# Four-block vision megakernel on one Trainium2 core: the channel norm moved into the projection's block and cut by bank, one ScalarE table set for logarithm and exponential, and image 1's delta sum taken per chunk inside its scan

## The reference

```python
x = x + L0(gn(x), ...)   # region normalization against bicubic maps
x = x + L1(gn(x), ...)   # 9-neighbour similarity graph, weighted sum, two 1x1 products
x = x + L2(gn(x), ...)   # Mamba block over the 4096 pixels as tokens
x = x + L3(gn(x), ...)   # deformable 3x3 convolution
```

```python
mu = mean(xf, -1); var = mean(square(xf - mu), -1)          # over the 32 channels of a token
xn = (xf - mu) * rsqrt(var + 1e-05) * ln_w + ln_b
xin, z = split(xn @ W_in.T)                                 # 64 + 64
u = silu(causal_conv4(xin) + conv_b)
dt, Bm, Cm = split(u @ W_xproj.T)                           # 2, 16, 16
delta = softplus(dt @ W_dt.T + b_dt)
# per token: h = exp(delta * A) * h + delta * u * B;  y = sum(h * C)
y = (ys + u * D) * silu(z);  out = y @ W_out.T
```

## Time and profile before

| | |
|---|---|
| runs | 1011.0 us median of 3 (1010.9 to 1011.95) |
| profiled execution | 1014.24 us, its span 1012.0 us |
| busy share of the span | PE 77%, VectorE 83%, POOL 57%, ScalarE 38% |
| mean granted TensorE clock | 0.832 of full speed |
| stages, us from the span's start | L0 to 50, L1 to 137, norm of L2 to 162, projection 0 to 205, scan 0 to 342, start of L3 to 368, projection 1 to 424, scan 1 to 671, L3 of image 1 to 1012 |

### The profile page before, as it was taken

The page is one execution under the profiler, slowest core; times in us unless marked ns, Lnnn a source line. Parts: engine busy times, 40 slices in busy tenths (PEclk is TensorE's granted clock), DMA queues, the critical chain, the costliest instruction groups (busy, mean ns, idle before and its releaser), DMA issues.

```text
span 1012.0 us, 8286 instructions
## 1 busy us (share of the span) xinstructions
PE 782.5 (77%) x2365; PEld 377.3 (37%) x2365; DVE 837.1 (83%) x1161; ACT 387.0 (38%) x544; POOL 580.1 (57%) x528
## 2 busy tenths in 40 slices
PE   2345875677787688676788787869379999999997
PEld 1132322222222124534454444423264444444443
DVE  3889842789999858879998899985989998979884
ACT  1120046854454136311212121101049586776650
POOL 0000000076765037877777777777777777777774
PEclk9666987979999889567777677776559999999998
DMA  5000017000000361111111111128353745444422
GB/s 122 0 0 1 0 31 155 17 0 1 1 1 0 64 133 49 37 52 53 51 50 52 52 49 53 51 64 195 110 139 90 195 136 143 122 123 130 120 65 53
DMA packets 32339, 69.82 MB, mean 69 GB/s; under 512 B 12368, under 2 KB 12624, under 8 KB 31184
## 3 DMA queue, kind: packets, MB, share of 16 engines
q1 hardware_dynamic: 16080, 35.27, 13.2%
q0 software_dynamic: 15360, 31.49, 12.1%
q10 hardware_dynamic: 864, 2.64, 1.2%
HBM read 54.94 MB, written 5.77 MB: 60 GB/s over the span
## 4 chain that ended last, share of the span: by engine, by line
PE 42%; DVE 26%; POOL 7%; issue 6%; ACT 2%; DMA 1%; DVEq 0%; ACTq 0%; POOLq 0%
PE PS L1481 19%; POOL got L780 7%; DVE scratch L1174 6%; PE PS L815 5%; DVE scratch L1100 4%; DVE scratch L1181 3%; PE PS L1057 2%; PE PS L1042 2%; PE PS L1498 2%; DVE prodg L791 2%; PE PS L855 2%; DVE PS L1097 2%; PE PS L1274 2%; DVE prodg L795 1%; PE PS L914 1%
## 5 line engine op out<-in xcount | busy, mean ns | idle before, releaser
L780 POOL DMA_INDIRECT got<-corner_table,idx_slot x405 | 402.8, 995 | 123.4 <-issue 123.4
L1042 PE MATMUL PS<-parts,selb 96*128 96x512 bf16 (+1 forms) x256 | 88.4, 446 | 85.0 <-DVE scratch L1100 45.3
L1057 PE MATMUL PS<-scratch,wt 128*128 128x512 f32 x256 | 146.1, 701 | 0.5 <-DVE scratch L1181 0.5
L1481 PE MATMUL PS<-scratch,UZ 128*128 128x512 f32 (+1 forms) x288 | 133.6, 613 | 2.9 <-DVE scratch L1466 2.9
L780 POOL DMA_INDIRECT got<-corner_table,idx_all x75 | 84.9, 1132 | 60.6 <-DVE prime L1348 38.0
L821 ACT ACTIVATE G<-PS 128x32 f32 (+1 forms) x32 | 6.3, 197 | 250.7 <-PE PS L815 250.6
L815 PE MATMUL PS<-ln_g,w 128*128 128x32 f32 x576 | 101.9, 344 | 0.0
L815 PEld LDWEIGHTS PS<-ln_g,w 128*128 128x128 f32 x576 | 99.3, 268 | 0.0
L1564 POOL MEMSET w<- 128x1152 f32 x1 | 1.1, 1058 | 159.7 <-POOLq L599 159.7
L1042 PEld LDWEIGHTS PS<-parts,selb 96*128 96x128 bf16 x256 | 22.9, 116 | 158.2 <-DVE scratch L1100 59.1
L1458 ACT ACTIVATE scratch<-UZ,knot 128x512 f32<-128x512 f32 (+1 forms) x128 | 81.6, 708 | 0.4
(11 more groups left out here) (350 smaller groups left out, 1354.8 us busy)
## 6 DMA issues: line engine op xcount, KB each, us to landing
UZ<-dense_rows SPq DMA_DIRECT2D x24, 512.0 KB, 4.1
got<-corner_table,idx_slot POOLq DMA_INDIRECT x405, 2.5
UZ<-dense_rows SPq DMA_DIRECT2D x96, 64.0 KB, 2.2
XN<-ln_g SPq DMA_DIRECT2D x6, 256.0 KB, 5.8
got<-corner_table,idx_all POOLq DMA_INDIRECT x75, 2.5
corner_table<-scratch SPq DMA_DIRECT2D x1, 1056.0 KB, 10.4
corner_table<-XN SPq DMA_DIRECT2D x1, 1056.0 KB, 10.4
X<-in_x SPq DMA_DIRECT2D x4, 256.0 KB
```

The source lines that it names most:

```text
L780: pool.indirect_dma_start(got[:, slot, tap, :, :].rearrange("p k c -> p (k c)"), None, tables[b], bass.IndirectOffsetOnAxis(ap=index[:, ta ...
L1042: last = nc.tensor.matmul(PS[:, first + n, :], selb[:, which, j, :], parts[:, bass.ds(i * CHUNK + n * BANK, BANK)], start=True, stop=True)
L1057: last = nc.tensor.matmul(PS[:, 4 + n, :], wt[:, W_SUM:W_SUM + P], dBC[:, j % 2, n * BANK:(n + 1) * BANK], start=False, stop=(j == PAIRS - 1))
L1481: last = nc.tensor.matmul(PS[:, n % 4, :], steps[rows, j, :, :].rearrange("p b c -> p (b c)"), ramps[k][rows, j, :], start=(j == 0), stop= ...
```

## The change

Three edits, and a small one at the program's start. The norm's block is gone: its five instruction lists become `norm_sync`, `norm_tensor`, `norm_scalar`, `norm_vector`, which stand first in the lists of the fourth block. Within them g is made in four passes, the banks are interleaved, and ScalarE takes logarithm and exponential of one bank before it goes on; its temporaries are in `scratch`. ScalarE is told which table set to load at the start, in the norm and in the projection (`preload_act_table_set`). Image 1's delta sum moves from the end of its projection to the start of each turn of its scan, and its logarithm's buffer from `scratch` (which the scan uses) to XN's second image.

```diff
@@ first block, ScalarE
+                    nc.scalar.preload_act_table_set("sqrt_and_others")
                     act.dma_start(vec[:, :], vecs).then_inc(vec_in, 16)
                     act.dma_start(mat[:, 0:M_PAIR, :], mats[:, 0:M_PAIR, :]).then_inc(mat_in, 16)
                     act.dma_start(patch[32:64, :, :], anchors).then_inc(vec_in, 16)
@@ the norm: the block and its buffers go, four functions come
+        sq = scratch[:, 0:HALF]
+        selw = scratch[0:96, HALF:2 * HALF]
...
+        def norm_sync(sp):
+            sp.dma_start(selw, sel).then_inc(ln["sel_in"], 16)
+            sp.wait_ge(ln["zeroed"], 1)
+            for k in range(2):
+                sp.wait_ge(ln["xn_ready"], 2 * k + 2)
+                load_part(sp, k, range(4 - 2 * k))
+            sp.wait_ge(ln["sel_in"], 16)
+
+        def norm_tensor(pe):
...
+            def center(n):
+                pe.wait_ge(ln["g_ready"], n + 1)
+                nc.tensor.matmul(PS[:, n, :], M(M_CENTER), g[:, n * BANK:(n + 1) * BANK], start=True,
+                                 stop=True).then_inc(ln["centered"], 1)
+
+            def mean(n):
+                pe.wait_ge(ln["squared"], n + 1)
+                if n == 3:
+                    pe.wait_ge(ln["w_done"], 1)
+                nc.tensor.matmul(PS[:, 4 + n, :], M(M_MEAN), sq_part(n), start=True, stop=True).then_inc(ln["var_done"], 1)
+
+            center(0), center(1), mean(0), center(2), mean(1), center(3), mean(2), mean(3)
+
+        def norm_scalar(act):
+            nc.scalar.activation(negA[:, :], V(V_A, PAIRS), ACT.Exp).then_inc(ln["expA_done"], 1)
+            act.wait_ge(ln["sqrt_go"], 1)
+            nc.scalar.activation(std[:, 0:1], std[:, 0:1], ACT.Sqrt).then_inc(ln["sqrt_done"], 1)
+            nc.scalar.preload_act_table_set("natural_log_exp_and_others")
...
+            def inverse(n):
+                act.wait_ge(ln["var_done"], n + 1)
+                nc.scalar.activation(sq_part(n), PS[:, 4 + n, :], ACT.Ln, bias=V(V_EPS)).then_inc(ln["std_done"], 1)
+                act.wait_ge(ln["std_done"], n + 1)
+                nc.scalar.activation(sq_part(n), sq_part(n), ACT.Exp, scale=-0.5).then_inc(ln["rstd_done"], 1)
...
+            square(0), square(1), inverse(0), square(2), inverse(1), affine(0), square(3), affine(1), inverse(2), inverse(3)
+            affine(2), affine(3)
+            act.wait_ge(ln["xn_ready"], 4)
+            load_part(act, 1, (2, 3))
+
+        def norm_vector(v):
...
+            for n in range(4):
+                cols = slice(n * BANK, (n + 1) * BANK)
+                nc.vector.tensor_scalar(g[:, cols], X[:, cols], rstd[:, 0:1], nmrs[:, :], ALU.mult, ALU.add).then_inc(ln["g_ready"], 1)
+            v.wait_ge(ln["g_ready"], 4)
...
+            for n in range(4):
+                v.wait_ge(ln["rstd_done"], n + 1)
+                nc.vector.tensor_tensor(sq_part(n), PS[:, n, :], sq_part(n), ALU.mult).then_inc(ln["normed"], 1)
+            v.wait_ge(ln["sel_in"], 16)
+            vchain(v, nc.vector.tensor_copy(selb[:, :, :, :].rearrange("p a b c -> p (a b c)"), selw))
@@
-        log_tmps = [got_flat[:, 0:L], chunk_buffer(4, 4)]
+        log_tmps = [got_flat[:, 0:L], XN[:, 1, :]]
@@ project_vector
                 left(3), low(2), low(3)
-                for c in range(NCHUNK):
-                    project_delta(v, 1, c)
@@ scan_scalar
+            act.wait_ge(pr["delta_ready"], c + 1)
@@ scan_vector
+            v.wait_ge(pr["v_ready"], c + 1)
+            v.wait_ge(pr["log_done"], c + 1)
+            tell(v, nc.vector.tensor_tensor(dl[:, tok], dl[:, tok], log_tmps[1][:, tok], ALU.add), pr["delta_ready"], c + 1)
             vchain(v, nc.vector.tensor_tensor(du, dl[:, tok], u[:, tok], ALU.mult))
@@ the fourth block's lists
+                norm_sync(sp)
                 load_tokens(sp, 0, 1, range(4))
...
+                norm_tensor(pe)
+                pe.wait_ge(ln["rstd_done"], 4)
+                pe.wait_ge(ln["normed"], 4)
                 project_tensor(pe, 0)
...
+                norm_scalar(act)
                 project_scalar(act, 0)
...
-                act.wait_ge(pr["delta_ready"], 8)
                 with nc.scalar.Fori(0, NCHUNK) as i:
...
+                norm_vector(v)
...
-                v.wait_ge(pr["delta_ready"], 8)
```

More of the change, by code:

```diff
@@ new lines, in norm_tensor @@
+        def norm_tensor(pe):
+            nc.tensor.matmul(PS[0:DI, 7, 0:P], wt[0:2, W_DTA:W_DTA + DI], wt[0:2, W_DTB:W_DTB + P],
+                             start=True, stop=True).then_inc(ln["dt_psum"], 1)
+            pe.wait_ge(ln["stats"], 1)
+            nc.tensor.matmul(PS[:, 0, 0:2], M(M_OWN), S2[:, :], start=True, stop=True).then_inc(ln["totals"], 1)
+            def center(n):
[8 more added lines that the diff above has]
+            center(0), center(1), mean(0), center(2), mean(1), center(3), mean(2), mean(3)
@@ new lines, in norm_vector @@
+        def norm_vector(v):
+            gn_partition_stats(v, banks_done=True).then_inc(ln["stats"], 1)
+            v.wait_ge(ln["totals"], 1)
+            vchain(v, nc.vector.tensor_copy(tot[:, 0:2], PS[:, 0, 0:2]))
+            variance(v, 1, GN_EPS).then_inc(ln["sqrt_go"], 1)
+            v.wait_ge(ln["sqrt_done"], 1)
+            vchain(v, nc.vector.reciprocal(rstd[:, 0:1], std[:, 0:1]))
+            vchain(v, nc.vector.scalar_tensor_tensor(nmrs[:, :], tot[:, 0:1], -1.0, rstd[:, 0:1], ALU.mult, ALU.mult))
+            for n in range(4):
+                cols = slice(n * BANK, (n + 1) * BANK)
+                nc.vector.tensor_scalar(g[:, cols], X[:, cols], rstd[:, 0:1], nmrs[:, :], ALU.mult, ALU.add).then_inc(ln["g_ready"], 1)
+            v.wait_ge(ln["g_ready"], 4)
+            tell(v, nc.vector.memset(XN[0:96, :, 0:3], 0.0), ln["zeroed"])
+            vchain(v, nc.vector.tensor_tensor(wx[:, :], wt[:, W_INX:W_INX + P], wt[:, W_CONV:W_CONV + P], ALU.mult))
+            vchain(v, nc.vector.tensor_scalar(bdt20[:, :], V(V_BDT), 20.0, None, ALU.subtract))
+            vchain(v, nc.vector.tensor_scalar(diagD[:, :], ident, V(V_D), None, ALU.mult))
+            v.wait_ge(ln["expA_done"], 1)
+            vchain(v, nc.vector.tensor_scalar(negA[:, :], negA[:, :], -1.0, None, ALU.mult))
+            v.wait_ge(ln["dt_psum"], 1)
+            vchain(v, nc.vector.memset(wdt[DI:P, :], 0.0))
+            tell(v, nc.vector.tensor_copy(wdt[0:DI, :], PS[0:DI, 7, 0:P]), ln["w_done"])
+            for n in range(4):
[3 more added lines that the diff above has]
+            vchain(v, nc.vector.tensor_copy(selb[:, :, :, :].rearrange("p a b c -> p (a b c)"), selw))
```

90 lines of the change are left out of this document (14 added, 76 removed).

## The result

Median of four runs: 1003.8 us (999.5 to 1006.4), against 1011.5 us for the kernel before on the same chip: ratio 0.9915, 95% interval 0.9888 to 0.9942. The same kernel run again beside others of this study gave 1003.9 us and 0.9908 (0.989 to 0.9926). The forecast was 1002.5 us, 997 to 1008, faster.

What follows compares the result with a forecast made beforehand. No engine bounds the whole; after 368 us POOL's gathers and VectorE with TensorE end within 1 us. +0.5 - 6.7 - 1.35 - 0.9 = -8.45, say 8.5, off the median 1011.0 gives 1002.5 us, range 997 to 1008.

Steps and rivals of the forecast that it cites:

- Start, +0.5: Program start: the preload's 1.28 us load may delay ScalarE's first transfers; 0.5 us slower, bounds 0 to +1.3.
- Norm, -6.7: Channel norm by bank: first projection product at 155.55 instead of 162.28, 6.7 us earlier; bounds 4.5 to 9.3.
- the handovers: Rival, 10%: in the norm, passing each bank alone between three engines costs 3 us; result 1005.5 us.
- TensorE did not keep its clock: Rival, 7%, denied here: TensorE keeps its high clock over the shorter gap before the projection; 2.6 us more gain, 999.9.
- the loads did not stay: Rival, 4%, denied here: norm's alternating logarithms and exponentials each reload a table, 1.28 us per change; 1011.6 or 1012.5 us.
- One set in the projection, -1.35: Image 0's projection: spared table load brings the first scan 1.35 us earlier; bounds 0 and 2.56; image 1: 0.
- Delta by chunk, -0.9: Image 1's delta sums moved into scan turns: 5.0 us gained by gathers, 4.1 lost in turns, net 0.9 gained.
- the freed gather: End of image 1's projection: without the burst of sums, the fifth and seventh gather groups come 5.0 us earlier.
- three times, 4.1 us: Image 1's scan: one sum between gate and product on VectorE costs 1.36 us in each of three later turns.
- The rival that the gather stays late: 10%: something other than image 1's delta sums held the gather, so moving them costs 4.1 us; result 1007.5 us.
- The clock rival: 6%: in image 1's scan TensorE's mean clock falls from 0.73 to 0.62, adding 11 us; result 1013.5 us.
- the first three rivals: Gather stays late (10%, 1007.5 us), handovers eat half of the norm's gain (10%, 1005.5), TensorE keeps its clock (7%, 999.9).

Runs made afterwards that it cites:

- the norm alone: Kernel before with only the norm by bank and its one preloaded set, delta sums in a row, logarithm's buffer moved: 1006.9 us, ratio 0.9938.
- sums back: Changed kernel with image 1's four delta sums back in a row at the end of its projection: 1005.8 us, ratio 0.9928 to the kernel before.
- the delta part alone: Kernel before with only image 1's delta sum moved to each scan turn and the logarithm's buffer moved: 1008.9 us, ratio 0.9964.
- the sums in the other form: Changed kernel with image 1's delta sums back in a row, each a scalar_tensor_tensor instead of a tensor_tensor: 1007.7 us, ratio 0.9935 to the kernel before.

## Why the prediction was right, point by point

- **Start, +0.5: wrong, 0.** It was taken from an open question, whether a transfer waits for the load. It doesn't (1.69 and 1.68 us), and the statistics of the image begin at 9.74 to 10.03 us in nine traces with the preload, at 9.64 to 10.35 in five without. The time alone can't tell 0.5 us from 0.
- **Norm, -6.7: right.** 22.0 became 15.2 us in the profiled execution, forecast 15.3, and the norm alone gave 6.3 us in the time (4.0 to 8.5). Over all traces it is 21.6 to 22.0 us with the old norm (three) and 15.15 to 15.85 with the new one (ten). Of the rivals, the handovers did not eat half of it; TensorE did not keep its clock (0.50 from 153.9 us on; first pair of products 1.83 and, in the second trace, 2.05 us; 2.05 before); the loads did not stay.
- **One set in the projection, -1.35: near it up to the first scan, less behind it.** 1.2 us by first product to first scan in most traces, with TensorE late next by 0.66 us as the last wait; at the first gather 0.6 are left on average. That TensorE would become the last wait was not in the sum. The time alone doesn't resolve it. The row decided rightly between 1.28 and 2.66 us: the Trainium skill, ScalarE: Activation LUTs, section What ACT_TABLE_LOAD costs, counts a drain of 1.38 us on top, and no trace here shows one: 112 of the 211 loads in the fourteen traces are followed by the next instruction within 0.04 us.
- **Delta by chunk, -0.9: mis-sized; alone it gave 3.6 us** (2.3 to 5.0). The first half, the freed gather, was right: 5.4 us of gathers' busy time went, the fifth group's wait fell under 1.5 us as said, and that group comes 4.2 us earlier against the first gather (5.0 forecast). The step that failed is the other half, "three times, 4.1 us" on the path. The price in the turn was right (3.80 us from gate to product, forecast 3.86; some 1.5 us a turn), but the end follows the gathers: by the traces the sums in the turns cost it some 2 us, and a second sum in each turn nothing that can be seen. The prediction had the reason in its own words, that behind 368 us a gain counts only if both chains get it, and it had the price on the other chain too: "POOL gains 5.0 less some 0.5 for each later sum", 3.5 us for three. It took the cost of VectorE's chain instead.
- **The rival that the gather stays late** fell: without the burst no gather was late. The prediction read the hold as ending with the burst; it ended at the first gap, and the gather 0.82 us behind that. The Trainium skill, SBUF — State Buffer, section Who interferes with whom, infers that a tensor_tensor doesn't stall descriptor generation; here a gather beside four in a row took 5.64 us (sums back) and 6.98 us (before), others 0.94. The prediction noted that the same section lets such a pass contend with a GpSimd instruction that reads SBUF; the gather reads its indices from there (idx_all), and the 0.94 us beside products with one input in PSUM fit that, but which of its reads or writes waits was not tested. The clock rival fell as well: the scan's mean clock is 0.75, 0.73 before:

```profile
414.00:655.00 241.00, 193.88 (x671) 110.32 (x671) 227.88 (x240) 39.91 (x53) 184.32 (x187) 0.75 0.19 51
```

**The sum.** Forecast -8.45; measured 0 - 6.3 - 1.2 (trace) - 3.6 = -11.1, with some 2.6 us of uncertainty; the whole change gave -8.6 and -9.3 by its two ratios. With the 0.6 us that the projection's part has left at the first gather, and the 1.9 us that undoing the delta part cost inside the changed kernel, it is -8.8. So parts and whole agree only within their errors, and that the total came out closer than its terms is in part luck. The chances of the forecast and the first three rivals add to 0.90, where the prediction has 0.88 for them and more; nothing hangs on it.

**The 14.5 us of the trace** contain luck. Of the 9.7 us ahead of the first gather, 1.9 lie ahead of the norm: its first statistic starts at 137.70 us before and at 135.83 after. That is no part of the change, as the delta part alone, with before's early stages, has it at 136.07, and five kernels that share the changed kernel's early stages or lack only the start's preload have it at 137.4 to 137.8 or 136.9. In all seven traces in which it is late TensorE's granted clock from 100 to 137 us is 0.95, in the seven early ones 1.00; early and late come with either form of the start and of the norm. Without these 1.9 there are 6.8 (norm) + 1.2 (projection) - 0.1 (image 0's scan and what follows it) = 7.9 us ahead of the first gather.

## What to carry to other kernels

Where two chains end together, write the end as a sum along each (here: first gather, gathers, gaps, tail) and book every term on its own chain: a cost counts by what it does to the chain that ends later (here 2 us of the 4.1 booked). Ask of a single long instruction what holds it before moving work: one wait between VectorE's passes gave 2.6 us where moving them gave 3.6. Where engines hand over whole tiles, the handing over by parts can be worth more (4.2 us here up to the first product) than the table loads beside it (2.6 with the split pass and the block's end); that the time shows this difference too is not shown.

## What the runs showed of the hardware that was not expected

- A gather on POOL that started beside four VectorE sums in a row, both inputs in SBUF, was held until the first gap between passes and ended 0.82 us later (6.98 and 5.64 us, others 0.94); a semaphore wait on the pass's own result is gap enough. The form with a scalar operand held it as well (6.98 us). Gathers beside products with one input in PSUM weren't held (0.94 to 0.95 us). Open: nine passes of 0.69 us in a row with both operands in SBUF, in the dense stage, hold gathers hardly at all (mean 0.97 us beside them, at most 1.44). What tells these from the four sums wasn't tried.
- A table load on ScalarE doesn't delay the transfers issued behind it: it began at 0.74 us, and the transfers were issued at 0.77, 1.21 and 1.69, as without it (0.74, 1.19, 1.68).
- Turns 2 to 4 of image 1's scan do the same work, yet one execution (the sums in the other form) has them at 61.8, 58.1 and 58.1 us. In the two traces of the changed kernel a longer turn is one in which VectorE waits for TensorE.
